# A two-layer sequence kernel: its weight generator's matmuls split into pairs of 64 rows and 32 columns, with a new step schedule

## The reference, cut to what matters

```
scale = cond @ norm_w.T + 1
h  = x * scale * rsqrt(mean(x*x))
u  = h @ up_w.T                      # 256 -> 2048, halves val and gate
h  = val * gelu(gate)
y  = quant(h) @ ternary(down_w).T    # 1024 -> 256
x  = y + x
dWd = (cond @ Wdd.T + bdd) * 0.1     # (128*256) outputs per sequence, from 64 inputs
dWu = (cond @ Wdu.T + bdu) * 0.1
down = relu(x @ (Wd + dWd).T + bd)
out  = x + down @ (Wu + dWu).T + bu
```

## Time and profile before

| | |
|---|---|
| median of 3 runs | 470.04 us (469.1 to 470.69) |
| the profiled execution | 469.12 us, its span 467.2 us |
| PE busy | 460.8 us, 99% of the span |
| DVE, ACT, POOL busy | 393.4, 366.1, 272.6 us |
| HBM read and written | 37.44 and 8.39 MB |

### The profile page before, as it was taken

One profiled execution on the slowest core, in us unless ns is written; L12 is line 12 of the kernel. 1 busy time (PEld: TensorE's weight loads), 2 busy tenths in 40 slices (PEclk: granted clock), 3 DMA queues, 4 the chain that ended last, 5 costly groups with the idle time before them and its releaser, 6 DMA issues.

```text
span 467.2 us, 10028 instructions
## 1 busy us (share of the span) xinstructions
PE 460.8 (99%) x3272; PEld 268.0 (57%) x3272; DVE 393.4 (84%) x785; ACT 366.1 (78%) x637; POOL 272.6 (58%) x682
## 2 busy tenths in 40 slices
PE   8999999999999999999999999999999999999996
PEld 6445656566565655555555555555555555555564
DVE  3988899999999988788888888888788888777886
ACT  4889999999999877776777677687686777677664
POOL 2237666866668654655756646656555756544674
PEclk9999999999999999999999999999999999999999
DMA  7954796897868536434454544555535465444343
GB/s 258 393 105 97 196 234 187 197 258 187 225 177 241 102 94 136 124 89 140 134 151 132 135 113 116 157 136 130 154 80 147 125 154 141 116 104 121 102 71 122
DMA packets 118003, 70.99 MB, mean 152 GB/s; under 512 B 102016, under 2 KB 102976, under 8 KB 115904
## 3 DMA queue, kind: packets, MB, share of 16 engines
q1 hardware_dynamic: 117504, 69.89, 57.0%
q10 hardware_dynamic: 448, 0.47, 0.3%
HBM read 37.44 MB, written 8.39 MB: 98 GB/s over the span
## 4 chain that ended last, share of the span: by engine, by line
PE 96%; DMA 1%; DVE 1%; ACT 1%; issue 0%; SPq 0%; DVEq 0%; ACTq 0%
PE bank L1189 68%; PE bank L1203 12%; PE bank L1269 5%; PE bank L1287 4%; PE bank L1301 4%; DMA adapt<-in_up_wT 1%; PE bank L1161 1%; PE bank L1171 1%; PE bank L1150 0%; PE bank L1215 0%; ACT up_hi L741 0%; ACT qn L663 0%; PE bank L1245 0%; DVE hid L944 0%; PE bank L1253 0%
## 5 line engine op out<-in xcount | busy, mean ns | idle before, releaser
L641 ACT ACTIVATE gel<-bank,rms 128x512 f32<-128x512 f32 x125 | 85.4, 684 | 83.6 <-PE bank L1189 82.1
L1189 PE MATMUL bank<-up_hi,xs_hi 128*128 128x512 f16 x492 | 146.3, 379 | 0.0
L1189 PE MATMUL bank<-up_lo,xs_hi 128*128 128x512 f16 x492 | 146.3, 379 | 0.0
L1189 PE MATMUL bank<-up_hi,xs_lo 128*128 128x512 f16 x492 | 146.3, 379 | 0.0
L890 DVE SCALAR_TENSOR_TENSOR hid<-bank,rms,gel 128x512 f32<-128x512 f32 x121 | 90.4, 748 | 49.7 <-ACT gel L641 49.0
L1189 PEld LDWEIGHTS bank<-up_lo,xs_hi 128*128 128x128 f16 x492 | 48.1, 98 | 58.1
L1189 PEld LDWEIGHTS bank<-up_hi,xs_lo 128*128 128x128 f16 x492 | 48.1, 98 | 58.0
L455 POOL TENSOR_TENSOR wsplit<-stage,wsplit 128x288 f16<-128x288 f32 x64 | 58.7, 949 | 30.0 <-ACT wsplit L611 29.9
L898 DVE TENSOR_REDUCE amax<-hid 128x1 f32<-128x1024 f32 x61 | 74.4, 1220 | 2.0
L654 ACT ACTIVATE hid<-hid,amax 128x1024 f32<-128x1024 f32 (+1 forms) x62 | 70.0, 1129 | 0.4 <-DVE amax L942 0.4
L466 POOL TENSOR_TENSOR nwt<-nwt 128x2 f32<-128x2 f32 x93 | 22.3, 240 | 79.0 <-DVE nwt L883 74.1
(11 more groups left out here) (153 smaller groups left out, 664.5 us busy)
## 6 DMA issues: line engine op xcount, KB each, us to landing
xT_s<-in_xT SPq DMA_DIRECT2D x32, 256.0 KB, 3.1
xn_s<-in_xn SPq DMA_DIRECT2D x32, 256.0 KB, 3.3
stage<-in_WddT SPq DMA_DIRECT2D x8, 1024.0 KB, 6.2
stage<-in_WduT SPq DMA_DIRECT2D x8, 1024.0 KB, 5.4
out<-out_s SPq DMA_DIRECT2D x30, 256.0 KB, 2.3
adapt<-in_up_wT SPq DMA_DIRECT2D x4, 512.0 KB, 6.6
x<-in_down_wT SPq DMA_DIRECT2D x2, 512.0 KB, 8.7
qT<-qn SPq DMA_TRANSPOSE x63, 2.7
```

Source lines behind the costliest of these rows:

```text
L641: nc.scalar.activation(gel_of(t, c), u_banks(t, c)[1][:], ACT.Gelu, scale=rms[:, t // TPB % XN_SLOTS, t % TPB:t % TPB + 1]).then_inc(gelu_ ...
L1189: ins = nc.tensor.matmul(dst[:], a[:, t // TPB % 2, k, cols], w[:, c, k, v, :], start=(k == 0 and n == 0), stop=(k == KD - 1 and n == 2))
```

## The change

`generate` no longer uses the zeros. Each matmul of 128 rows and 64 columns becomes two of 64 rows and 32 columns, one on the upper and one on the lower half of the partitions, which write different PSUM banks: 96 matmuls and 96 weight loads for a chunk instead of 48. Both halves of a chunk are then complete only at its end, so there is one wait ahead of the chunk, for `evacuate(q - 1, 0)`, and both evacuations wait for the whole chunk.

The schedule changes with it. Chunks go to steps 5 to 8, 10 to 13, 15 to 18 and 20 to 23. `ADAPT` is 26, 27, 28, 29, 31, ... instead of 24, 26, 27, 28, 30, ...: two steps later for b = 0, one step later for b = 1 to 26, and the same for b = 27 to 31. `split_step`, `split_tiles` and `biases` follow it. On DVE the two evacuations move ahead of `residual` and `total`. The layout of the adapters in SBUF is plain now, so `ad_views` reads without a rearrangement, and the last operation of `base_sum` is done in two pieces, which bring the base weights into that layout.

```diff
-CHUNK_STEP = [FIRST + 1 + q for q in range(NGEN)]
+CHUNK_STEP = [FIRST + 1 + q + q // 4 for q in range(NGEN)]
-    return max(2 * b + 7, CHUNK_STEP[-1] + 4 + (4 * b + 2) // 3)
+    return max(2 * b + 7, CHUNK_STEP[-1] + 2 + max(1, (4 * b + 2) // 3))
+def split_step(b):
+    if b < 2:
+        return CHUNK_STEP[-1] + 2
+    if b == AD_SLOTS:
+        return ADAPT[0] + 2
+    return min(ADAPT[b] - 2, NT - 4 + b - (B - 4)) if b < LAST_B else NT - 2
 def adapter_splits(s):
-    return [b for b in range(B) if (min(ADAPT[b] - 2, NT - 4 + b - (B - 4)) if b < LAST_B else NT - 2) == s]
+    return [b for b in range(B) if split_step(b) == s]
+def biases(s):
+    return [b for b in range(B) if min(ADAPT[b], 2 * b + X1_SLOTS + 2) == s]
 def split_tiles(s):
-    return [t for t in range(NT) if max(ADAPT[t // TPB] - 4 + t % TPB, t + DOWN) == s]
+    return [t for t in range(NT) if max(ADAPT[t // TPB] - 4 + t % TPB, t + DOWN,
+                                        ADAPT[max(t // TPB - X1T_SLOTS, 0)] + t % TPB if t // TPB >= X1T_SLOTS else 0) == s]
...
-                nc.gpsimd.tensor_scalar(base[:], base[:], A_SCALE, None, ALU.mult).then_inc(base_ready, 1)
+                for w in range(2):
+                    nc.gpsimd.tensor_scalar(
+                        base[:, w].rearrange("p (h x m) -> p h x m", h=2, m=BCH),
+                        bias_raw[:, w].rearrange("p (x h m) -> p h x m", h=2, m=BCH),
+                        A_SCALE, None, ALU.mult).then_inc(base_ready, 1)
...
-                for b in sequences(s, 0):
+                for b in biases(s):
                     output_bias(b)
...
             def evacuate(q, n):
-                dve.wait_ge(gen_full, 2 * q + n + 1)
+                dve.wait_ge(gen_full, 2 * q + 2)
...
+                for q in chunk(s, 2):
+                    evacuate(q, 0)
+                    evacuate(q, 1)
                 for t in residuals(s):
                     residual(t)
...
-                for q in chunk(s, 2):
-                    evacuate(q, 0)
-                    evacuate(q, 1)
...
-                for n in range(2):
-                    after(pe, gen_done, 2 * q + n - 2)
-                    for m in range(BCH):
-                        dst = gen_ps[(2 * q + n) % 3][:].rearrange("p (h m b) -> p m h b", h=2, m=BCH)[:, m]
-                        cols = slice((n * BCH + m) * P, (n * BCH + m + 1) * P)
-                        passes = ((0, cdiag_hi), (0, cdiag_lo), (1, cdiag_hi))
-                        for k, (part, moving) in enumerate(passes):
-                            ins = nc.tensor.matmul(dst, wsplit[:, q % 2, part, cols], moving[:],
+                after(pe, gen_done, 2 * q - 1)
+                for m in range(GCH):
+                    cols = slice(m * P, (m + 1) * P)
+                    passes = ((0, cdiag_hi), (0, cdiag_lo), (1, cdiag_hi))
+                    for k, (part, moving) in enumerate(passes):
+                        for half in range(2):
+                            rows = slice(half * C, (half + 1) * C)
+                            ins = nc.tensor.matmul(gen_ps[(2 * q + half) % 3][:, m * B:(m + 1) * B],
+                                                   wsplit[rows, q % 2, part, cols], moving[rows, half],
                                                    start=(k == 0), stop=(k == len(passes) - 1))
-                    ins.then_inc(gen_full, 1)
+                            if m == GCH - 1 and k == len(passes) - 1:
+                                ins.then_inc(gen_full, 1)
```

More of the change, by code:

```diff
@@ L336, in ad_views @@
         def ad_views(b, w):
-            src = adapt[:, w, b, :].rearrange("p (x h m) -> p h x m", h=2, x=NBK)
-            hi, lo = (part[:, w].rearrange("p (h x m) -> p h x m", h=2, x=NBK) for part in ad_parts(b))
-            return src, hi, lo
+            hi, lo = (part[:, w] for part in ad_parts(b))
+            return adapt[:, w, b, :], hi, lo
         def ad_parts(b):
@@ L534, in base_sum @@
                 pool.wait_ge(base_ready, 1)
-                nc.gpsimd.tensor_tensor(base[:], base[:], bias_raw, ALU.add).then_inc(base_ready, 1)
+                nc.gpsimd.tensor_tensor(bias_raw, base[:], bias_raw, ALU.add).then_inc(base_ready, 1)
                 pool.wait_ge(base_ready, 2)
-                nc.gpsimd.tensor_scalar(base[:], base[:], A_SCALE, None, ALU.mult).then_inc(base_ready, 1)
+                for w in range(2):
[3 more added lines that the diff above has]
+                        A_SCALE, None, ALU.mult).then_inc(base_ready, 1)
             def split_cond():
@@ L826, in evacuate @@
                 w = q // NGC
-                at = (q % NGC * 2 + n) * 2 * BCH
+                at = n * P + q % NGC * GCH
                 if q == 0:
-                    dve.wait_ge(base_ready, 3)
-                dve.wait_ge(gen_full, 2 * q + n + 1)
+                    dve.wait_ge(base_ready, 4)
+                dve.wait_ge(gen_full, 2 * q + 2)
                 nc.vector.scalar_tensor_tensor(
-                    out=adapt[:, w, :, at:at + 2 * BCH].rearrange("p b m -> p m b"),
+                    out=adapt[:, w, :, at:at + GCH].rearrange("p b m -> p m b"),
                     in0=gen_ps[(2 * q + n) % 3][:].rearrange("p (m b) -> p m b", b=B),
                     scalar=DELTA_SCALE * A_SCALE / (W_SCALE * C_SCALE),
-                    in1=base[:, w, at:at + 2 * BCH].unsqueeze(2).to_broadcast([P, 2 * BCH, B]),
+                    in1=base[:, w, at:at + GCH].unsqueeze(2).to_broadcast([P, GCH, B]),
                     op0=ALU.mult, op1=ALU.add).then_inc(gen_done, 1)
```

## The result

The changed kernel takes 483.47 us (median of 4 runs, 479.77 to 483.80) against 469.88 us of the kernel before (4 runs): a ratio of 1.0275, with an interval of 1.0254 to 1.0295. The forecast was 469.0 us, with a range to 473.5; the change costs 13.6 us instead. The profiled execution took 483.76 us, its span 482.0, which is 14.8 us more than the span before. The quickest of the four, 479.77 us, has a mean granted clock of 0.995, the other three 0.992; only one of those three has a trace.

What follows compares the result with a forecast made beforehand. PE was taken as the bound, with ACT and DVE 3% behind. PE would save 8.3 us, the chain ACT, low part, gate, evacuation give back 7.3, other edits cost nothing: 470.04 - 1.0 = 469.0 us, range 463.5 to 473.5.

Steps and rivals of the forecast that it cites:

- c: PE's time for the 96 matmuls of a chunk: 0.88 us forecast, against 1.40 us for the old chunk.
- The premise that the blocks overlap: In the generator, the two 64-row blocks run at the same time on PE: 18.3 ns a pair.
- the continued line: PE's matmul price, 1/2.4 ns a column plus 2.5 ns, seen down to 64 columns and extended to 32.
- pairs overlap, but cost what one costs now: Rival on the generator's pairs: c of 1.40 to 1.52, a loss of 1.6 to 3.5 us; chance 0.11.
- The sentence on the 60 cycles: Skill page's matmul overhead of about 60 cycles: 25 ns a generator matmul, 1.20 us a chunk if pairs overlap.
- the 0.163 that the prediction feared: Possible PE drain in us when the matmul shape changes; two a chunk would bring c to 1.21, no gain.
- the prediction's own formula: Time of four chunk steps and a free one: 34.97 + c, or 30.91 + 4c by PE alone; now 35.85 us.
- The other edits, at nothing: Later residual and adapters, loads, base weights in two operations and plain adapter layout were to cost no time.
- POOL's low part: Ends 6.62 us after gelu(s, 1) starts, so PE waits 0.66 us before the generator behind a free step.
- The chain ACT, low part, gate, evacuation: Path to the fourth generator's start in each group; was to give back 7.3 of PE's 8.3 us saving.
- the 1.35 at which the prediction lets PE alone decide: Value of c in us from which PE's own work, not the chain, sets a group's time.
- 7.26: Length in us forecast for a chunk step, from DVE's average from low part to low part.

Runs made afterwards that it cites:

- e1: Kernel before (48 matmuls of 128 rows, old adapter layout) with only the new schedule and order on DVE: 474.77 us, ratio 1.0119.
- e4: Changed kernel with a chunk's 48 matmuls of the upper rows first, then the 48 of the lower: 492.27 us in one run.
- e8: Changed kernel with all 128 rows in each of a chunk's 96 matmuls, still 32 columns each: 489.31 us in one run.
- e5: Changed kernel with 8 tiny matmuls more at its start, 32 more PE instructions: 479.76 us, ratio 1.0204.
- e6: Changed kernel with 18 tiny matmuls more at its start, 72 more PE instructions: 480.83 us, ratio 1.0233.
- e7: e2 with 8 tiny matmuls more at its start, 32 more PE instructions: 470.72 us, ratio 1.0010.
- e3: Changed kernel with chunks 2 to 15 loaded in a sixteenth of their columns and not scaled again by ACT: 476.87 us, ratio 1.0150.
- e11: Changed kernel with the load of chunk q issued only when generate(q - 2) has ended on PE: 477.98 us, ratio 1.0182.
- e12: e2 with the load of chunk q issued only when generate(q - 2) has ended on PE: 472.63 us, ratio 1.0057.
- e2: Changed kernel with the old steps for chunks and adapters, evacuations still ahead of the residual: 474.00 us, ratio 1.0073.
- e10: e2 with a load wait on a generator one step too early, so loads did not move; a repeat of e2: 474.54 us, ratio 1.0131.
- e9: Changed kernel with a load wait on a generator one step too early, so loads did not move; a repeat: 480.40 us, ratio 1.0228.

## Why the prediction was wrong

**The term c was mis-sized.** The prediction took 0.88 us a chunk, "18.3 ns a pair"; it measured 1.40. The timeline of the changed kernel shows the first and last pair of a chunk, and the next `up` (start, us):

```profile
56.73 0.19 PE L1292 MATMUL bank<-cdiag_hi,wsplit 64*128 64x32 f16 x2
...
57.90 0.19 PE L1292 MATMUL bank<-cdiag_hi,wsplit 64*128 64x32 f16 x2
58.03 0.61 PE L1211 MATMUL bank<-up_hi,xs_hi 128*128 128x512 f16 x2
```

1.17 us over 47 distances is 24.9 ns a pair, and 0.10 us passes before `up`; 0.10 stands ahead of the chunk too. The premise that the blocks overlap was right, and the continued line was wrong: it has a floor at 25 ns. The rival "pairs overlap, but cost what one costs now", with c = 1.40 to 1.52 and a chance of 0.11, is what happened. The Trainium skill, "TensorE: Matmul & The Clock Gate", section "Wait — 56ns, not 53.3ns?", states this floor of about 25 ns for 32 columns, from one matmul's start to the next; here the trace has 24.9 ns a pair, so two matmuls on different rows share it. The sentence on the 60 cycles in the prediction gave 1.20 us, to which the runs add 0.2 for the changes of rows. The drain that the Trainium skill, "TensorEngine Tiling (Array Packing)", section Key Properties, describes fits those 0.10 us at either end, less than the 0.163 that the prediction feared.

**A whole resource was left out.** By the prediction's own formula c = 1.40 gives a loss of 1.6 us. Of the 14.8, 10.4 come from two stalls that no step and no rival of it contains: PE's supply of instructions. The change was costed in time on the array, while its count, 192 instructions in 1.2 us where there were 96 in 1.4, was read off and not costed: an undisturbed chunk step gives PE 266 instructions (132 and 134 in its window), more than a block, where it was 163 (82 and 81). Shown by the runs: the stalls need the doubled count (e1 has none, e4 and e8 have one), sit at one place in a block (e5, e6), move or go when the count is shifted (e5 to e7), and go as long ones when the loads are taken away (e3) or moved (e11, e12). That the fetch waits behind the load's packets is seen in the traces of the long stalls (the changed kernel, e2, e10); when it is asked for no trace shows.

**"The other edits, at nothing" was wrong.** e1 costs 4.8 us (in its profiled run 0.8 is a late start) where the formula has 1.6. Right in it: the first chunk behind a free step waits for POOL's low part; forecast 0.66, measured 0.85, 0.45, 0.85. The views of waits call it `issue`, but the low part ends at 87.51 + 3.65 = 91.16 us and the chunk starts at 91.25:

```profile
87.51 3.65 POOL L471 TENSOR_TENSOR wsplit<-stage,wsplit 128x288 f16<-128x288 f32 x4 [7.50 <-ACT wsplit L632]
```

Not in it: the evacuations moved ahead put `scaled_low`, which stands behind them on DVE, late by 0.4 us twice; and the adapters' move puts two `residual_low` casts (0.73 us) into step 23, where DVE is the chain already, so the last chunk waits for an evacuation, 0.3 us in the changed kernel and 0.7 to 1.7 in e1, e3, e5, e6 and e11. No run takes these two edits back one by one; they are read from the chains.

**The chain ACT, low part, gate, evacuation** did not decide: with c over the 1.35 at which the prediction lets PE alone decide, PE has no idle time ahead of most chunks, and steps are 7.45 us. Whether 7.26 is right for a smaller c stays untested.

Open: why one stall spares the next chunks, and why runs of one program (e2, e7, and e9 beside the changed kernel) differ by whether and where they stall, and by how late the step loop starts.

## What to carry to other kernels

Count instructions, not only columns: splitting 64 columns into two matmuls of 32 left the time of a chunk as it was and doubled what PE must be sent. Where hundreds of short matmuls run in a burst beside large loads, look in the trace for idle time of PE named "issue" in the middle of a run of matmuls, and for the count of instruction packets. Before moving work into another step, ask on each engine what stands behind it in that step.

## What the hardware showed unexpectedly

PE ran out of instructions. The packet that ended the first stall is seen in the DMA view of the stretch from 61.2 to 62.4 us, that of the second between 176.7 and 177.8:

```profile
q8 instruction: 1, 0.02, 4.9%
...
q8 instruction: 1, 0.02, 5.7%
```

4.9% of 16 engines over 1.2 us is 0.94 us on one of them, and PE goes on at 63.75, 1.4 us behind its landing at 62.33 (1.5 at the second stall). So most of the stall isn't the transfer, but its late start (4.7 us behind the chunk's first matmul) and the restart.

What a stall costs depends on the clock behind it: 3.39 us idle cost 5.26 with the matmuls at the 1.2 GHz level behind it, and e6's 1.87 us was followed by an `up` of 2.59 us at full speed, while behind e3's 1.6 us it took 4.40. What decides between the last two the runs don't show.
